# A message-passing kernel: the first half of the filter layer ahead of the sums, in layer 0

## The chip, the cores and the metric

The kernel runs on one core of a Trainium2 chip. The metric is the device time of one execution in microseconds. The engines are TensorE (PE in the profile, its weight loads PEld), VectorE (DVE), ScalarE (ACT), GpSimd (POOL) and SyncE (SP); they run side by side and order themselves with semaphores only.

## What is computed

A graph of 12,500 nodes and 412,500 edges, sorted by destination, goes through two layers. The part that matters here:

```python
# layer 0
msg = edge_weight[:, None] * x[src]
agg = segment_sum(msg, dst, num_segments=N)
h = relu((x + agg) @ W1 + b1)
x = layernorm(x + (h @ W2 + b2))
# layer 1, on the new x
h1 = x @ lin1_w.T
z = softplus(edge_attr @ nn_w1.T + nn_b1) - log(2)      # "filter layer 1": depends on the edges alone
W = (softplus(z @ nn_w2.T + nn_b2) - log(2)) * c[:, None]
msg = W * h1[dst]                                       # summed over src
```

The first filter layer doesn't depend on `x`, so the kernel computes it during layer 0's pass over the edges and stores it for layer 1.

## The kernel before

**Stages.** After some preparation comes the pass over the edges of layer 0, in T = 403 tiles of 1024 edges, then layer 0's node stage, then the pass over the edges of layer 1 and its node stage. The change lies in the first pass alone (the engines' programs from line 352 on). The edges are sorted by destination, so a tile touches few nodes; a "window" is 42 nodes (WIN), and each tile runs an inner loop over its windows (one for each tile with these inputs: a tile issues eight gathers per window, and 3224 are issued).

**What each engine does in tile t**, in the order of its program; each engine works off its own queue in order:

- *GpSimd* (L420 to 437): for each window eight indirect gathers (`xg[s]`, s = 0 to 7, 128 rows of `x` each, L432). Gather s waits until the indices `gidx` are there and until the sum that read `xg[s]` in the window before is over (`summed`). Each `xg[s]` is one buffer.
- *ScalarE* (L402 to 416): copies the indices `gidx` for the window's gathers in two halves (L411), each when the gathers of the window before that used that half have landed; then `soft_1(t, 0)` and `soft_1(t, 1)` (L395, L397, L399: Abs, Exp, Ln), on the filter results of tile t-1.
- *TensorE* (L454 to 481): the counts (L463, L465: sixteen small bf16 matmuls on `oha`, which VectorE makes at the start of its tile; `counted`); then the window loop: wait for `flushed` and for the one-hots, and eight sums (L475), each after its gather has landed, into `bank[0]`, each an increment of `summed`. Then the two halves of the first filter layer (L481), `attr` times `nn1`, 512 columns in fp32 each, into `bank[2]` and `bank[3]` (`z1_set`). Half h waits for the tile's `attr` load and for `hid_set >= taken_up(t, h)`: VectorE's `hidden(t, h)` must have read the bank's last contents.
- *VectorE* (L545 to 596): `rel`, `oha`; in the window loop it waits for all sums of the window before, makes eight one-hots (L563), adds `bank[0]` of the window before to `aggT` (L499), and steps `rel`; then the ranks of the tile: `pair` (L574), `ahead` (L578, which waits for the counts), `count` (L580, L584), `seen` (L582), `rank` (L587); then `hidden(t, 0)` (L506), a bucket count (L699, in three of four parts), and `hidden(t, 1)`. Each `hidden` combines the filter result of tile t-1 with ScalarE's output and increments `hid_set`.
- *SyncE* (L366 to 376): loads `attr` for tile t (L371) when both halves of t-1 are done; stores `hid` (L363) when `hidden(t, 1)` is done; clears a block of the table for layer 1 (L376).

`attr`, `hid`, the one-hots and each bank named above are single buffers. The counts of what is before: `z1_set` starts at 2 by two matmuls on zeros, `hid_set` at 2, `summed` at 8. From these, `made(k, h)` = 2k + h + 1 and `taken_up(k, h)` = 2k + h + 3.

Of the kernel before, what the change touches and what calls it, by code (L numbers as in the profile page):

```python
# [51 lines left out]
def edge_network_kernel(nc, x_rows, x_cols, src_cols, dst_cols, w_cols, dst_rows,  # L52
# [8 lines left out]
    with ctx:  # L61
        def sb(name, shape, dt):
            return ctx.enter_context(nc.sbuf_tensor(name, shape, dt))

        def sem(name):
            return ctx.enter_context(nc.semaphore(name))
# [45 lines left out]
        nn1 = sb("nn1", [P, D], f32)  # L112
        b1c = sb("b1c", [P, 1], f32)
        bank = [ctx.enter_context(nc.psum_tensor(f"bank{i}", [P, 512], f32)) for i in range(8)]
# [6 lines left out]
        with ExitStack() as c0:  # L121
# [28 lines left out]
            with nc.Block() as block:  # L150
                @block.sync
                def _(sp):
                    for i in range(NGRP):
                        sp.dma_start(rows_i[0:g[i], i, :], dst_rows[P * i:P * i + g[i], :]).then_inc(dst_in[i], 16)
                    sp.dma_start(wgt[:, :], w_cols).then_inc(w_in, 16)
                    sp.wait_ge(s_win, 1)
                    sp.dma_start(base_d[:, :].rearrange("(i p) o -> p i o", p=P), least[:, :].rearrange("p (i o) -> p i o", o=1), allow_slow_non_contiguous=True).then_inc(win_st, 16)
                    sp.dma_start(nwin_d[:, :].rearrange("(i p) o -> p i o", p=P), most[:, :].rearrange("p (i o) -> p i o", o=1), allow_slow_non_contiguous=True).then_inc(win_st, 16)
                    sp.wait_ge(win_st, 32)
                    sp.dma_start(base[:, 0:T], base_d[0:T, :].rearrange("t o -> o t").broadcast_to([P, T])).then_inc(s_tab, 16)  # L160
                    sp.dma_start(nwin[:, 0:T], nwin_d[0:T, :].rearrange("t o -> o t").broadcast_to([P, T])).then_inc(s_tab, 16)
                    for i in range(NGRP):
                        sp.wait_ge(dst_half, i + 1)
                        sp.dma_start(dst16[P * i:P * i + g[i], :], rows_h[0:g[i], i, :]).then_inc(s_st, 16)
                    sp.wait_ge(s_st, 16 * NGRP)
                    sp.wait_ge(s_tab, 32)
# [137 lines left out]
        with ExitStack() as c1:  # L304
# [3 lines left out]
            with ExitStack() as c2:  # L308
                def sb2(name, shape, dt):
                    return c2.enter_context(nc.sbuf_tensor(name, shape, dt))  # L310
# [9 lines left out]
                attr = sb2("attr", [P, 2, HE], f32)  # L320
# [17 lines left out]
                attr_padded, attr_in = sem("attr_padded"), sem("attr_in")  # L338
                z1_set, abs1, exp1, ln1, hid_set = (sem(n) for n in ("z1_set", "abs1", "exp1", "ln1", "hid_set"))
# [8 lines left out]
                def taken_up(k, h):  # L348

                    return 2 * k + h + 3  # L350

                with nc.Block() as block:
# [85 lines left out]
                    @block.tensor  # L438
                    def _(pe):
                        def plan_part(q):  # L440

                            pe.wait_ge(bucket_counts, NB + q * PT)
                            nc.tensor.matmul(bank[5][0:NB, 0:1], counts[:, 0:NB], ones[:, 0:1], start=True, stop=True).then_inc(planned, 1)
                            pe.wait_ge(plan, PLAN_STEPS * q + 3)
                            nc.tensor.matmul(bank[5][:, 128:128 + NB], blocks[0:NB, :], before_col[0:NB, :], start=True, stop=True)
                            nc.tensor.matmul(bank[5][:, 256:256 + NB], blocks[0:NB, :], upto[0:NB, :], start=True, stop=True)
                            nc.tensor.matmul(bank[5][0:NB, 384:385], upto[0:NB, :], blocks[0:NB, 0:1], start=True, stop=True).then_inc(planned, 1)
                            pe.wait_ge(plan, PLAN_STEPS * q + 5)
                            nc.tensor.matmul(bank[4][:, 0:SLOTS], ones16[0:NB, :], at_or_past[0:NB, :], start=True, stop=True).then_inc(planned, 1)

                        nc.tensor.matmul(bank[0][:, 0:WIN], lower[:, :], zero16[:, 0:WIN], start=True, stop=True).then_inc(summed, SUB)
                        for h in range(2):
                            nc.tensor.matmul(bank[2 + h][:, :], ident[:, :], zero[:, 0:HE], start=True, stop=True).then_inc(z1_set, 1)
                        pe.sem_inc(counted, 1)  # L454
                        jobs = TileTable(pe, "pe0", nwin)
                        for q, first, past_last in parts:
                            plan_part(q)
                            with pe.Fori(first, past_last) as t:
                                windows = jobs.windows()
                                pe.wait_ge(oha_set, t + 1)  # L460
                                pe.wait_ge(seen_set, t + 1)
                                for s in range(SUB):
                                    nc.tensor.matmul(above, lower[:, :], oha[:, s, :], start=(s == 0), stop=(s == SUB - 1))  # L463
                                for s in range(SUB):
                                    ins = nc.tensor.matmul(in_tile, ones16[:, :], oha[:, s, :], start=(s == 0), stop=(s == SUB - 1))  # L465
                                ins.then_inc(counted, 1)
                                with pe.Fori(0, windows):
                                    j = jobs.number()
                                    pe.wait_ge(flushed, j + 2)
                                    pe.wait_ge(onehot_ready, j + 1)  # L470
                                    for s in range(SUB):
                                        if s == HALF:
                                            jobs.read_ahead(t)
                                        pe.wait_ge(gathered[s], 16 * (j + 2))
                                        nc.tensor.matmul(bank[0][:, 0:WIN], xg[s][:, :], onehot[:, s, :],  # L475
                                                         start=(s == 0), stop=(s == SUB - 1)).then_inc(summed, 1)
                                    jobs.step()
                                for h in range(2):
                                    pe.wait_ge(attr_in, 16 * (t + 1))
                                    pe.wait_ge(hid_set, taken_up(t, h))  # L480
                                    nc.tensor.matmul(bank[2 + h][:, :], nn1[:, :], attr[:, h, :], start=True, stop=True).then_inc(z1_set, 1)  # L481

                    @block.vector
                    def _(dve):
# [973 lines left out]
```

## Time and profile before

| | |
|---|---|
| Median of 3 runs | 9315.23 us (9307.72 to 9319.87) |
| The profiled execution | 9315.85 us, of which the span is 9314.2 us |
| Busy, share of the span | PE 65%, PEld 52%, DVE 70%, ACT 37%, POOL 68% |
| Layer 0's gathers | 3224, from 158.0 to 4368.7 us of the span |
| TensorE's mean granted clock | 0.74 of full speed; 0.70 from 1000 to 4000 us |
| DMA | 1533 MB, mean 165 GB/s |

Shares of busy time are means over stages with different limits, so the rows below are of the stage that the change touches. In them PE matmuls are grouped with their neighbours of the same kind ("x6" is six, or three fp32 products of two passes each), times are us from the start of the span, and a bracket at the end of a line is the idle time of that engine just before it and what ended it.

### The profile page before, as it was taken

Reading aid. Unit: us, or ns where it says so; the run is one execution under the profiler, and the core shown is the slowest. Engines: PE = TensorE matmul, PEld = TensorE weight load, DVE = VectorE, ACT = ScalarE, POOL = GpSimd, SP = SyncE. Lnnn points to the kernel's source line nnn. Section 1 sums busy time; section 2 is a strip of 40 time slices with the busy share of each in tenths; the row PEclk is TensorE's granted clock in tenths of the full one; section 3 lists DMA queues with packets and bytes.
Section 4 is the critical chain, followed back from the end, with each engine's and each line's share of the span. In section 5 each row is a group of like instructions: output and inputs, shape, how many; then the busy total and the mean of one; then the engine's idle time right before and its main releaser. Section 6 shows DMA issues by size and latency. Waiting matters only on the chain. (4 is left out here: it accounts for less than half of the span.)

```text
span 9314.2 us, 204001 instructions
## 1 busy us (share of the span) xinstructions
PE 6033.2 (65%) x35189; PEld 4808.1 (52%) x35190; DVE 6494.6 (70%) x20428; ACT 3471.8 (37%) x6781; POOL 6297.2 (68%) x6541
## 2 busy tenths in 40 slices
PE   2666666666666666666655556666666666666676
PEld 1444444444444444444444446666666666666665
DVE  7777777777777776665655556777777777777655
ACT  2333333333333333333544443333333333333202
POOL 2777777777777777775277777777777777777400
PEclk8676766776767667776855557888888888888887
DMA  3444444444444444444444446666666666666554
GB/s 101 148 146 147 148 144 146 149 146 143 146 149 147 145 145 148 149 147 142 143 134 134 134 134 199 208 210 206 205 206 208 209 207 206 205 207 207 174 167 147
DMA packets 803241, 1533.30 MB, mean 165 GB/s; under 512 B 193070, under 2 KB 206820, under 8 KB 802707
## 3 DMA queue, kind: packets, MB, share of 16 engines
q1 hardware_dynamic: 593415, 1093.58, 36.2%
q0 software_dynamic: 209456, 436.16, 15.7%
q10 hardware_dynamic: 348, 3.33, 0.1%
q14 instruction: 16, 0.13, 0.0%
q8 instruction: 6, 0.10, 0.0%
HBM read 967.92 MB, written 564.58 MB: 165 GB/s over the span
## 5 line engine op out<-in xcount | busy, mean ns | idle before, releaser
L1204 POOL DMA_INDIRECT sorted_messages<-rows,sidx x3224 | 3212.4, 996 | 1154.7 <-issue 932.4
L432 POOL DMA_INDIRECT xg<-x_rows,gidx x3224 | 3043.0, 944 | 1306.8 <-issue 1020.2
L475 PE MATMUL bank<-onehot,xg 128*128 128x42 f32 x6448 | 1116.6, 326 | 1400.4 <-DMA xg<-x_rows,gidx 1386.2
L475 PEld LDWEIGHTS bank<-onehot,xg 128*128 128x128 f32 x6448 | 1004.2, 233 | 1474.0 <-DMA xg<-x_rows,gidx 1457.1
L1132 PE MATMUL bank<-hot,block_rows 128*128 128x128 f32 x9312 | 1576.2, 347 | 145.4 <-DVE hot L1286 145.1
L1132 PEld LDWEIGHTS bank<-hot,block_rows 128*128 128x128 f32 x9312 | 1530.3, 260 | 169.2 <-issue 154.0
L481 PE MATMUL bank<-attr,nn 128*128 128x512 f32 x1612 | 1453.7, 1057 | 3.0 <-DVE hid L506 3.0
L1102 PE MATMUL bank<-w_nn2T,e_hid 128*128 128x128 f32 x6448 | 1039.0, 314 | 162.2 <-DMA e_hid<-hidden 162.1
L1102 PEld LDWEIGHTS bank<-w_nn2T,e_hid 128*128 128x128 f32 x6448 | 1007.8, 226 | 245.3 <-DMA e_hid<-hidden 212.1
L1113 PE MATMUL bank<-h1w,ohT 128*128 128x128 bf16 x3224 | 349.4, 275 | 1069.6 <-DVE ohT L1233 1066.4
L1257 DVE SCALAR_TENSOR_TENSOR rows<-filt,meta,bank 128x128 f32<-128x128 f32 x3224 | 904.7, 343 | 94.7 <-DVE filt L1248 47.2
L563 DVE TENSOR_SCALAR onehot<-cols,rel,wgt 128x42 f32<-128x42 f32 x3224 | 734.8, 327 | 233.2 <-PE bank L475 230.5
L1286 DVE TENSOR_TENSOR hot<-cols,block_rows 128x512 f32<-128x512 f32 x1167 | 800.2, 686 | 118.0 <-DMA block_rows<-sorted_messages 117.5
L1113 PEld LDWEIGHTS bank<-h1w,ohT 128*128 128x128 bf16 x3224 | 266.7, 123 | 1144.4 <-issue 1144.2
L395 ACT ACTIVATE soft<-bank 128x512 f32<-128x512 f32 x808 | 474.8, 588 | 1008.5 <-PE bank L481 1004.0
L1166 ACT ACTIVATE rows<-meta 128x4 f32 (+1 forms) x806 | 167.4, 208 | 1743.0 <-DMA sorted_messages<-rows,sidx 1743.0
L1248 DVE SCALAR_TENSOR_TENSOR filt<-bank,soft 128x512 f32<-128x512 f32 x806 | 555.0, 689 | 344.7 <-issue 188.3
L1157 ACT ACTIVATE soft<-bank 128x512 f32<-128x512 f32 x806 | 481.2, 597 | 734.9 <-PE bank L1102 553.3
L411 ACT ACTIVATE gidx<-srci 128x4 int32 x806 | 165.5, 205 | 1543.2 <-DMA xg<-x_rows,gidx 1357.7
L481 PEld LDWEIGHTS bank<-attr,nn 128*128 128x128 f32 x1612 | 483.2, 329 | 422.5 <-issue 411.4
L1297 DVE TENSOR_TENSOR aggT<-aggT,bank 128x128 f32 x1164 | 328.9, 283 | 435.6 <-issue 258.9
L506 DVE SCALAR_TENSOR_TENSOR hid<-bank,soft 128x512 f32<-128x512 f32 x808 | 542.9, 682 | 4.6 <-ACT soft L399 4.6
(180 smaller groups left out, 7427.8 us busy)
## 6 DMA issues: line engine op xcount, KB each, us to landing
block_rows<-sorted_messages SPq DMA_DIRECT2D x389, 792.0 KB
hidden<-hid SPq DMA_DIRECT2D x404, 512.0 KB
e_hid<-hidden SPq DMA_DIRECT2D x403, 512.0 KB
sorted_messages<-zero SPq DMA_DIRECT2D x403, 264.0 KB
dstb<-dst SPq DMA_DIRECT2D x403, 256.0 KB
attr<-attr_cols SPq DMA_DIRECT2D x403, 204.0 KB
xg<-x_rows,gidx POOLq DMA_INDIRECT x3224, 4.2
sorted_messages<-rows,sidx POOLq DMA_INDIRECT x3224
```

The source lines that it names most:

```text
L432: pool.indirect_dma_start(xg[s][:, :], None, x_rows, bass.IndirectOffsetOnAxis(ap=gidx[s // HALF][:, s % HALF:s % HALF + 1], axis=0),).the ...
L475: nc.tensor.matmul(bank[0][:, 0:WIN], xg[s][:, :], onehot[:, s, :], start=(s == 0), stop=(s == SUB - 1)).then_inc(summed, 1)
L481: nc.tensor.matmul(bank[2 + h][:, :], nn1[:, :], attr[:, h, :], start=True, stop=True).then_inc(z1_set, 1)
L506: dve.scalar_tensor_tensor(hid[:, h, :], bank[2 + h][:, :], 0.0, soft1[h][:, :], ALU.max, ALU.add).then_inc(hid_set, 1)
L563: ins = dve.tensor_scalar(onehot[:, s, :], cols[:, 0:WIN], rel[:, s:s + 1], wgt[:, ds(here + s, 1)], ALU.is_equal, ALU.mult)
L1102: ins = nc.tensor.matmul(bank[2 + h][:, s * P:s * P + P], hid[:, h, s * P:s * P + P], nn2T[:, :], start=False, stop=(s == HALF - 1))
L1113: ins = nc.tensor.matmul(bank[4 + h][:, s * P:s * P + P], ohT[:, at:at + P], h1w[:, :], start=True, stop=True)
L1132: ins = nc.tensor.matmul(sums[u][:, 0:P], block_rows[k][:, u, s, 0:D], hot[u][:, s, :], start=(s == 0), stop=(s == HALF - 1))
L1204: pool.indirect_dma_start(table, bass.IndirectOffsetOnAxis(ap=sidx[b][h][:, s:s + 1], axis=0), rows[b][h][:, s, :], None).then_inc(landed[ ...
L1248: dve.scalar_tensor_tensor(filt[h][:, :], bank[2 + h][:, :], 0.0, soft2[h][:, :], ALU.max, ALU.add).then_inc(filt_set, 1)
L1257: ins = dve.scalar_tensor_tensor(rows[b][h][:, s, 0:D], filt[h][:, part], meta[:, ds(here + (h * HALF + s), 1), 1], bank[4 + h][:, part], ...
L1286: dve.tensor_tensor(hot[u][:, :, :], cols[:, :].rearrange("p (o n) -> p o n", o=1).broadcast_to([P, HALF, P]), block_rows[k][:, u, :, D:D ...
```

## The change

TensorE's first filter layer is put into a function, and half 0 is issued right after the tile's counts, ahead of the window loop with the sums of gathered rows. Half 1 stays behind the sums. Each half takes its two waits with it. Nothing else differs.

```diff
+                        def first_layer(t, h):
+
+                            pe.wait_ge(attr_in, 16 * (t + 1))
+                            pe.wait_ge(hid_set, taken_up(t, h))
+                            nc.tensor.matmul(bank[2 + h][:, :], nn1[:, :], attr[:, h, :], start=True, stop=True).then_inc(z1_set, 1)
+
...
                                 ins.then_inc(counted, 1)
+                                first_layer(t, 0)
                                 with pe.Fori(0, windows):
                                     j = jobs.number()
                                     pe.wait_ge(flushed, j + 2)
...
                                     jobs.step()
-                                for h in range(2):
-                                    pe.wait_ge(attr_in, 16 * (t + 1))
-                                    pe.wait_ge(hid_set, taken_up(t, h))
-                                    nc.tensor.matmul(bank[2 + h][:, :], nn1[:, :], attr[:, h, :], start=True, stop=True).then_inc(z1_set, 1)
+                                first_layer(t, 1)
```

## Rows read from the trace of the kernel before

**Rows 1.** The gathers' line, 1000 to 4000 us: count, durations, landing.

```profile
L432 POOL DMA_INDIRECT xg<-x_rows,gidx x2300: 938/944/1000, 999.4 to 3999.4; - x192
...
DMA to landing us min/median/max: 2.4/4.1/7.2
```

**Rows 2.** The page's group of the same line, over the whole span.

```profile
L432 POOL DMA_INDIRECT xg<-x_rows,gidx x3224 | 3043.0, 944 | 1306.8 <-issue 1020.2
```

**Rows 3.** Waits, 1000 to 4000 us: total us, times, longest us.

```profile
PE bank L475 <- DMA xg<-x_rows,gidx: 991.9, 387, 4.6
...
ACT soft L395 <- PE bank L481: 713.6, 286, 7.9
...
PEld bank L481 <- DVE hid L506: 5.5, 6, 1.2
```

**Rows 4.** Timeline, 2000 to 2022 us, all engines: start, length, engine, line.

```profile
2004.59 1.51 PE L475 MATMUL bank<-onehot,xg 128*128 128x42 f32 x6 [3.09 <-DMA xg<-x_rows,gidx]
...
2005.89 3.34 PE L481 MATMUL bank<-attr,nn 128*128 128x512 f32 x4
...
2006.24 1.78 DVE L563 TENSOR_SCALAR onehot<-cols,rel,wgt 128x42 f32<-128x42 f32 x8 [0.81 <-PE bank L475]
...
2009.12 0.22 DVE L574 TENSOR_TENSOR pair<-bucket 128x64 f32 x1 [0.90 <-issue]
...
2009.41 0.33 SPq L371 DMA_DIRECT2D attr<-attr_cols  x1
...
2009.79 1.34 PE L475 MATMUL bank<-onehot,xg 128*128 128x42 f32 x10
...
2009.99 0.27 DVE L578 TENSOR_TENSOR bank<-bank,seen 128x100 f32<-128x100 f32 x1 [0.64 <-PE bank L465]
...
2011.93 0.94 POOL L432 DMA_INDIRECT xg<-x_rows,gidx  x1 [0.30 <-issue]
2012.17 0.20 ACT L411 ACTIVATE gidx<-srci 128x4 int32 x1 [0.46 <-issue]
2012.61 0.68 DVE L506 SCALAR_TENSOR_TENSOR hid<-bank,soft 128x512 f32<-128x512 f32 x1
...
2013.27 0.94 POOL L432 DMA_INDIRECT xg<-x_rows,gidx  x1 [0.40 <-issue]
...
2015.21 1.27 PE L475 MATMUL bank<-onehot,xg 128*128 128x42 f32 x6 [4.08 <-DMA xg<-x_rows,gidx]
...
2015.76 0.20 ACT L411 ACTIVATE gidx<-srci 128x4 int32 x1 [3.38 <-DMA xg<-x_rows,gidx]
```

**Rows 5.** Timeline, 170 to 275 us: the first tile, where TensorE waited for `hid`.

```profile
174.53 3.64 PE L475 MATMUL bank<-onehot,xg 128*128 128x42 f32 x16 [8.84 <-DVE aggT L499]
...
175.24 0.23 DVE L574 TENSOR_TENSOR pair<-bucket 128x64 f32 x1 [0.86 <-issue]
...
175.99 0.94 POOL L432 DMA_INDIRECT xg<-x_rows,gidx  x1 [8.11 <-PE bank L475]
...
178.03 0.68 DVE L506 SCALAR_TENSOR_TENSOR hid<-bank,soft 128x512 f32<-128x512 f32 x1
...
178.77 3.78 PE L481 MATMUL bank<-attr,nn 128*128 128x512 f32 x4 [0.60 <-DVE hid L506]
```

**Rows 6.** Busy time by stretch: PE, PEld, DVE, ACT, POOL, then granted PEclk.

```profile
2008.00:2009.00 1.00, 1.00 (x2) 0.22 (x2) 0.23 (x3) 0.97 (x2) 0.82 (x1) 0.66 0.55 197
...
2015.00:2016.00 1.00, 0.79 (x5) 0.79 (x6) 0.89 (x1) 0.20 (x1) 0.69 (x2) 0.75 0.20 62
```

**Rows 7.** DMA queues, 2014.0 to 2014.5 us: packets, MB, share of 16 engines.

```profile
q1 hardware_dynamic: 4, 0.01, 5.8%
```

## Prediction

> **What bounds the kernel now.** I read the gathers' own line first, then the table of waits, then one tile in order of time. The reader is to see one stage, the pass over the edges in layer 0. [rows 1] has 2300 gathers from 999.4 to 3999.4 us; at eight to a tile of 1024 edges that is 3000.0 / 2299 x 8 = **10.44 us per tile**. The whole kernel issues 3224 of them [rows 2], 403 tiles of one window each. A gather is 0.94 us and its issue gap 0.30 us [rows 1, 4], so the GpSimd stream alone would take 8 x 1.25 = 10.0 us; the rest is its short waits. [rows 3] says who waits in those 287.5 tiles: TensorE stands 991.9 us for gathered rows (3.4 us a tile), ScalarE 713.6 us for the filter layer (2.5 us a tile), and TensorE almost never for `hid` (5.5 us in all). That last row is the one that the change touches.
>
> [rows 4] is one tile, t. TensorE ends the sums of t-1 at 2004.59 + 1.51 = 2006.10, runs both filter matmuls of t-1 (from 2005.89, 3.34 us), then the counts of t, and at 2009.79 five of the eight sums of t, whose rows are there. Then it idles 4.08 us until the last three arrive at 2015.21. VectorE starts the one-hots of t at 2006.24, 0.14 us after the sums of t-1, goes through add, `pair` (2009.12), `ahead`, `count`, `rank`, and only at 2012.61 reaches `hidden(t, 0)`, which ends at 2013.29. GpSimd's gathers for t+1 begin at 2013.27; the buffers had been free since the five sums.
>
> **What changes, part by part.** Nothing is added or removed: 403 first-half filter matmuls (fp32, 512 columns) move past the sums, with both their waits. (a) `attr_in` for t: see (d). (b) `hid_set >= taken_up(t, 0)`, which is 2t + 3 with 2 given at the start: it is reached by `hidden(t, 0)` of the same tile, not of the one before. VectorE comes to it at the end of its tile. So TensorE, done with the counts before 2009.99 (where `ahead` is released [rows 4]), would stand until 2013.29, and **behind it in its queue stand all eight sums of t**. Who waits for those: GpSimd (each gather of t+1 needs its buffer back) and VectorE (the one-hots of t+1 need all sums of t).
>
> (c) That closes a ring which before was open: sums(t-1) -> VectorE's whole tile up to `hidden(t, 0)` -> first filter matmul -> sums(t). Its length:
> - sums end to one-hots: 0.14 us (2006.10 to 2006.24 [rows 4]).
> - one-hots to `pair`: 2.88 us (2006.24 to 2009.12 [rows 4]).
> - `pair` to the end of `hidden(t, 0)`: in the tile of [rows 4] it contains a wait for the counts; in [rows 5], where there was none, it is 175.24 to 178.03 + 0.68, 3.47 us. I take this one, as the counts will follow a single filter matmul and come in time.
> - `hid` to TensorE: 178.71 to 178.77, 0.06 us [rows 5].
> - first filter matmul: half of the pair, between 3.34 / 2 [rows 4] and 3.78 / 2 [rows 5] at the low clock; 1.8 us. At full clock about 0.9.
> - eight sums: 16 matmuls in 3.64 us at the low clock [rows 5], 0.455 us a sum; at the full clock ten in 1.34 us [rows 4], 0.27 us a sum. Which of them? The burst of [rows 4] starts at 2004.59 after an idle stretch; the granted clock is 0.66 over 2008 to 2009 [rows 6], that is 0.5 (1.2 GHz) to about 2008.7 and then 1.0 (2.4 GHz): 4.1 us from the start of the burst. In the changed kernel the burst begins with the filter matmul after about as long an idle stretch; so 1.8 us of filter, 2.3 us or five sums at the low clock, three at the full: 1.8 + 2.3 + 0.8 = 4.9 us. Bounds: 0.9 + 2.2 = 3.1 (all full), 1.8 + 3.64 = 5.4 (all low).
>
> Sum: 0.14 + 2.88 + 3.47 + 0.06 + 4.9 = **11.45 us per tile**; bounds 9.65 and 12.0.
>
> A second ring goes through GpSimd and two tiles. From the end of sums(t-1) the first sum of t is over after 0.14 + 2.88 + 3.47 + 0.06 + 1.8 + 0.45 = 8.8 us. A gather held by a sum starts 1.0 us after it (sum over at 174.53 + 0.455, gather at 175.99 [rows 5]); held by `gidx`, 0.9 us (2012.37 to 2013.27 [rows 4]). The eighth starts 7 x 1.25 = 8.75 us later, lands after 3.8 us (2011.93 to ScalarE's `gidx` at 2015.76 [rows 4]; the median of all is 4.1 [rows 1]), and its sum takes 0.3 to 0.45. Two tiles are 8.8 + 1.0 + 8.75 + 3.83 + 0.4 = 22.8 us, **11.4 a tile**; 10.9 with the filter matmul and the sums at the full clock.
>
> Two rings of equal length, with landings from 2.4 to 7.2 us [rows 1], give more than either: I add 0.2 us, an estimate, and take **11.65 us per tile**.
>
> (d) The other waits. The load of `attr` is issued once both halves of the tile before are done (2009.41 in [rows 4], 0.18 us after the pair's end at 2009.23); its queue, q1, still has 4 packets at 2014.0 to 2014.5 [rows 7], so it lands about 4.9 us after issue. In the changed kernel: sums end + 0.9 (1.8 if the clock is low) + 0.2 + 4.9 = 6.0 to 6.9, against 6.55 at which `hid` comes. Usually hidden by VectorE's tile; with a low clock it adds 0.35 us. It is past no other DMA on SP's queue, as store, clearing and load keep their order. ScalarE gains: its 2.5 us wait for the first half [rows 3] goes, since that result is there before the gathers land. What is late next is not ScalarE but the sums, so this is worth nothing. The second half keeps its place; `hidden(t, 1)` has ended 1.7 us after `hidden(t, 0)`, long before it. Other stages don't change.
>
> **The sum.** (11.65 - 10.44) x 403 = 488 us. The profiled execution took 9315.85 us (span 9314.2), level with the median of the runs, 9315.23; so 9315.85 + 488 = **9804 us**, 5.2% slower.
>
> **Rivals.**
> 1. *The clock stays full* through the burst. TensorE's idle stretch might shrink or shift so that the fall after it (clock 0.75 over 2015 to 2016, so falling just as the burst starts, [rows 6]) doesn't come. Then the VectorE ring is 9.65, the GpSimd ring 10.9 us a tile and decides: 9315.85 + 0.46 x 403 = 9500 us. Against it: idle is 11.6 less some 7 us of work, over 4 us, as now. The Trainium skill, "TensorE: Matmul & The Clock Gate", section "Why this matters for your kernels", tells us to avoid long TensorE gaps between bursts to hold the clock; by it a filter matmul set into the gap could pay. In [rows 4] the matmul can't start until the gap is nearly over.
> 2. *The clock stays low* through the sums and `attr` is late: 12.0 + 0.35 = 12.35 us, 9315.85 + 1.91 x 403 = 10,086 us. For it: the sums stream only 42 columns and are short; against it, the clock rose in bursts that held such sums.
> 3. *Faster.* ScalarE's 2.5 us freed, `gidx` is ready early, and GpSimd runs without waits at 10.0 to 10.1 us a tile: 9315.85 - 0.35 x 403 = 9175 us. It decides if `hidden(t, 0)` ends before TensorE has done the counts, at or before 2009.99; it ends 3.3 us after.
> 4. *No change*: the 1.8 us fit into TensorE's idle 4.08 us, 2013.35 to 2015.15, just ahead of the last three sums, 9316 us. It would hold if GpSimd had spare buffers; but its gather for t+1 at 2013.27 needs the first sum of t, which would end only at 2015.6.
>
> **How the numbers follow.** Forecast (11.3 to 12.0 us a tile, 9662 to 9944 us) 0.68; rival 1 0.12; rival 2 0.13; rival 3 0.04; rival 4 0.03. The range leaves out the two last and the upper part of rival 2: 9490 to 10,060. Within 0.2%, about what a measurement can tell from no change, 0.03; faster 0.04; slower 0.93.
>
> **What would show it.** In the changed kernel's rows: TensorE waits for `hid` (VectorE line of `hidden`) some 3 to 4 us a tile, and for gathers little; all eight sums stand together after a filter matmul; GpSimd waits for the sums about 1.2 us a tile; ScalarE's wait for the filter layer goes down; gathers are 11.3 to 12.0 us apart by eights, and the time from the last gather to the end is unchanged. Wrong would be: TensorE's wait for `hid` small, or GpSimd still at 1.25 us throughout.

## The result and the profile after

The changed kernel takes **10311.48 us** (10300.55 to 10323.45) against 9317.55 us for the kernel before, a ratio of 1.107 with a 95% interval of 1.105 to 1.108. The direction was right, the size was not: 994 us more where 488 were forecast, and outside the range.

The profile after, the page: the groups of the gathers and of the filter layer (now L455).

```profile
L432 POOL DMA_INDIRECT xg<-x_rows,gidx x3224 | 3042.2, 944 | 2296.5 <-PE bank L482 1515.5
...
L455 PE MATMUL bank<-attr,nn 128*128 128x512 f32 x1612 | 1662.3, 1135 | 1768.2 <-DMA attr<-attr_cols 1578.3
```

The gathers are as long as in [rows 2]; GpSimd's idle time before them has grown from 1306.8 to 2296.5 us, by 989.7 us, and the span has grown by 989.3 us (10303.5 against 9314.2). The whole loss is in this one stage.

The gathers' line of the changed kernel, 1000 to 4000 us, to set beside [rows 1]:

```profile
L432 POOL DMA_INDIRECT xg<-x_rows,gidx x1857: 938/944/971, 999.9 to 3999.3; - x186
```

Eight gathers are (3999.3 - 999.9) / 1856 x 8 = **12.93 us** apart, against 10.44 before; 2.49 x 403 = 1003 us. (All periods below are worked out in this way.)

The waits of the same stretch, for [rows 3]:

```profile
PE bank L455 <- DMA attr<-attr_cols: 960.0, 220, 5.3
POOL xg L432 <- PE bank L482: 877.0, 682, 10.3
DVE onehot L567 <- PE bank L482: 873.3, 231, 4.6
PEld bank L455 <- DVE hid L510: 775.2, 173, 5.5
```

TensorE no longer waits for gathered rows: the table has no such row for it. It waits some 4 us a tile ahead of the first half, and the rows disagree on whom for: its weight load is released by `hid`, the matmul itself by the `attr` load, which came last in 220 of 232 tiles. GpSimd and VectorE wait for the sums.

One tile of the changed kernel, timeline 2000 to 2030 us, for [rows 4]:

```profile
2004.16 3.48 PE L482 MATMUL bank<-onehot,xg 128*128 128x42 f32 x16
...
2007.43 2.06 PE L455 MATMUL bank<-attr,nn 128*128 128x512 f32 x2
...
2009.67 0.32 SPq L371 DMA_DIRECT2D attr<-attr_cols  x1
...
2013.54 0.68 DVE L510 SCALAR_TENSOR_TENSOR hid<-bank,soft 128x512 f32<-128x512 f32 x1
...
2014.98 2.07 PE L455 MATMUL bank<-attr,nn 128*128 128x512 f32 x2 [4.15 <-DMA attr<-attr_cols]
...
2016.84 3.48 PE L482 MATMUL bank<-onehot,xg 128*128 128x42 f32 x16
```

This is the ring, with all its links: sums end 2007.64; 2.03 us of second half until the load goes out; 5.31 us until the first half starts; 1.86 us until the sums start; 3.48 us of sums, ending at 2020.32. Sum **12.68 us**; the stage's mean of 12.93 holds longer loads too (the next one goes out at 2022.35, and TensorE starts at 2028.33, 5.98 us later). `hid` is ready at 2014.22, 0.76 us before the first half starts: the forecast's VectorE ring is there, but the load closes a longer one around it.

The granted clock through that burst (columns as in [rows 6]):

```profile
2009.00:2010.00 1.00, 1.00 (x10) 0.72 (x9) 0.84 (x5) 0.47 (x1) 0.79 (x1) 0.50 0.24 66
...
2011.00:2012.00 1.00, 0.00 (x0) 0.00 (x0) 1.00 (x4) 0.45 (x1) 0.70 (x2) 0.73 0.32 66
...
2013.00:2014.00 1.00, 0.00 (x0) 0.00 (x0) 1.00 (x2) 0.00 (x0) 0.90 (x1) 1.00 0.39 127
```

TensorE's work from 2002.30 to 2010.8 runs wholly at 0.5 (1.2 GHz). In this tile the clock rises to 1.0 (2.4 GHz) in 2011 to 2012, when the burst is over, and is high while TensorE waits; in the next wait, from 2023.6 to 2028.3, it stays at 0.50. Why it differs is open. The low clock in the bursts isn't this tile's alone. The durations of all 1612 filter matmuls (two make a half; ns, min/median/max), the kernel before and then the changed one:

```profile
L481 PE MATMUL bank<-attr,nn x1612: 593/1061/1222, 178.8 to 4376.0; 128*128 128x512 f32 x180
```

```profile
L455 PE MATMUL bank<-attr,nn x1612: 1057/1087/1223, 178.2 to 5364.9; 128*128 128x512 f32 x180
```

The short ones, run at the high clock, are gone: none is under 1057 ns.

### The profile page after: what moved, and what is told of

Same layout as the page of the kernel before. It is cut to its first block and busy times, and to the rows that moved or that the text cites. A ratio compares the mean times of both kernels' runs of the same rounds, so it can differ in the third digit from the quotient of the medians.

```text
span 10303.5 us, 204001 instructions
## 1 busy us (share of the span) xinstructions
PE 6657.4 (65%) x35189; PEld 5383.8 (52%) x35190; DVE 6501.5 (63%) x20428; ACT 3518.0 (34%) x6781; POOL 6302.5 (61%) x6541
## 5 line engine op out<-in xcount | busy, mean ns | idle before, releaser
L432 POOL DMA_INDIRECT xg<-x_rows,gidx x3224 | 3042.2, 944 | 2296.5 <-PE bank L482 1515.5
L455 PE MATMUL bank<-attr,nn 128*128 128x512 f32 x1612 | 1662.3, 1135 | 1768.2 <-DMA attr<-attr_cols 1578.3
L482 PEld LDWEIGHTS bank<-onehot,xg 128*128 128x128 f32 x6448 | 1475.0, 334 | 416.3 <-issue 416.3
L482 PE MATMUL bank<-onehot,xg 128*128 128x42 f32 x6448 | 1402.2, 411 | 0.0
L455 PEld LDWEIGHTS bank<-attr,nn 128*128 128x128 f32 x1612 | 422.3, 322 | 1848.9 <-DVE hid L510 1492.2
L469 PEld LDWEIGHTS bank<-oha,lower 128*128 128x128 bf16 x3224 | 322.3, 147 | 499.1 <-issue 486.4
```

The source lines that it names most:

```text
L432: pool.indirect_dma_start(xg[s][:, :], None, x_rows, bass.IndirectOffsetOnAxis(ap=gidx[s // HALF][:, s % HALF:s % HALF + 1], axis=0),).the ...
```

## The experiments

Three things were to be told apart: the wait for `hid`, the wait for the `attr` load, and the clock. The kernel before ran beside each group of experiments and had medians from 9300 to 9353 us, so kernels of different groups are compared by their ratios; a point is 1% of the kernel before, 93 us. The groups are the change; e1 to e4; e5 to e8; e9 and e10; e11; e12; e13 and e14.

| kernel | us | ratio to before, 95% interval |
|---|---|---|
| the change | 10311 | 1.1067 (1.1053 to 1.1081) |
| e1 split load | 9962 | 1.0662 (1.0644 to 1.0680) |
| e2 added matmuls | 9810 | 1.0502 (1.0481 to 1.0523) |
| e3 split load, added matmuls | 9513 | 1.0182 (1.0165 to 1.0199) |
| e4 both halves ahead | 10634 | 1.1382 (1.1363 to 1.1401) |
| e5 second bank | 10346 | 1.1074 (1.1050 to 1.1098) |
| e6 second bank, split load | 9343 | 0.9995 (0.9984 to 1.0006) |
| e7 split load, `hidden` early | 9426 | 1.0074 (1.0053 to 1.0096) |
| e8 before, added matmuls | 9679 | 1.0359 (1.0328 to 1.0390) |
| e9 e6, load earlier | 9167 | 0.9795 (0.9782 to 0.9809) |
| e10 e9, three added matmuls | 9172 | 0.9805 (0.9792 to 0.9819) |
| e11 e9's loads, order of before | 9538 | 1.0207 (1.0193 to 1.0221) |
| e12 e11, store not held | 9189 | 0.9834 (0.9812 to 0.9856) |
| e13 e3 with half the added work | 9631 | 1.0352 (1.0336 to 1.0367) |
| e14 before, split load | 9235 | 0.9931 (0.9918 to 0.9945) |

### e1: the load of half 0 earlier

The semaphore `attr_in` becomes one for each half, and TensorE's wait ahead of half h goes by `attr_in[h]`. SyncE's part:

```diff
-                                sp.wait_ge(z1_set, made(t, 1))
-                                sp.dma_start(attr[0:GAUSS + 1, :, :].rearrange("a h e -> a (h e)"), attr_cols[:, ds(t * TE, TE)]).then_inc(attr_in, 16)
+                                for h in range(2):
+                                    sp.wait_ge(z1_set, made(t, h))
+                                    sp.dma_start(attr[0:GAUSS + 1, h, :], attr_cols[:, ds(t * TE + h * HE, HE)]).then_inc(attr_in[h], 16)
```

> The changed kernel, with the attr load split in two: half 0 for tile t is loaded as soon as the first filter matmul of t-1 is done, some 5 us before half 1. In the changed kernel TensorE starts the first half 0.76 us after hid is there (2014.22 to 2014.98), and the wait ends with the attr load. Theory attr (the load is the last to come): the first half starts with hid, and the ring at the low clock is 0.14 + 6.44 + 0.06 + 1.86 + 3.48 = 12.0 us a tile instead of 12.93, so 10311 - 0.93 x 403 = 9940 us. Theory VectorE (hid alone holds it, the load comes just with it): no change, 10311 us. The clock stays at 0.5 in the bursts in both.

Measured 9962 us; the theory of the load had said 9940. The waits of e1, 1000 to 4000 us:

```profile
PE bank L456 <- DVE hid L511: 891.3, 249, 5.1
```

Now `hid` ends the wait in all 249 tiles, and gathers by eights are 12.06 us apart, which is the forecast's VectorE ring with the clock low (12.0). The load was worth 12.93 - 12.06 = 0.87 us a tile, 350 us, or 4.05 points by the ratios.

### e2 and e3: the clock

```diff
                                 ins.then_inc(counted, 1)
+                                for k in range(8):
+                                    nc.tensor.matmul(bank[1][:, :], ones16[:, :], bucket16[:, 0:HE], start=True, stop=True)
                                 first_layer(t, 0)
```

> The changed kernel, with eight bf16 matmuls of 512 columns on TensorE after the counts, into a bank that nobody reads, in the 4 us in which it waits for hid and attr. Theory clock (half of the loss is that the burst runs at 1.2 GHz): the granted clock of the stage goes from 0.57 to over 0.9, the first half takes 0.9 us instead of 1.86, a sum 0.27 instead of 0.43, the attr load is issued 0.9 us earlier; the VectorE ring is 0.14 + 6.44 + 0.06 + 3.1 = 9.75 us and GpSimd's two-tile ring gives 10.5 to 10.9: 9340 to 9500 us. Theory ring (the clock matters little beside the waits): within 100 us of 10311. If the added matmuls hold the clock but come in the way of the first half, 0.2 to 0.5 us a tile more.

> Both edits. Theory clock and ring: with the clock full GpSimd's two-tile ring decides, so the split load adds next to nothing, 9300 to 9480 us. Theory attr as the larger part: below the fill alone by over 200 us.

Measured 9810 and 9513 us. The added work is eight bf16 matmuls of 512 columns whose results nobody reads. It does nothing but keep TensorE busy in part of its wait, and takes 5.65 points off the changed kernel and 448 us, 4.8 points, off e1. The stretch 1000 to 4000 us of the changed kernel, of e2 and of e3, in that order:

```profile
1000.00:4000.00 3000.00, 1970.98 (x8372) 1400.83 (x8371) 1853.54 (x5130) 956.43 (x1856) 1751.82 (x1857) 0.57 0.36 118
```

```profile
1000.00:4000.00 3000.00, 2224.38 (x11052) 1440.58 (x11279) 2019.45 (x5611) 1048.55 (x2045) 1933.12 (x2045) 0.76 0.41 130
```

```profile
1000.00:4000.00 3000.00, 2267.47 (x11865) 1463.92 (x12115) 2147.83 (x5982) 1119.34 (x2199) 2076.55 (x2196) 0.79 0.45 140
```

The mean clock goes from 0.57 to 0.76 and 0.79. It did not reach the expected 0.9, and neither time the 9340 to 9500 that went with it: in e2's timeline the first half takes 1.12 us and the second, behind the sums, again 2.05.

```profile
2003.39 1.12 PE L455 MATMUL bank<-attr,nn 128*128 128x512 f32 x2 [3.56 <-DMA attr<-attr_cols]
...
2008.33 2.05 PE L455 MATMUL bank<-attr,nn 128*128 128x512 f32 x2
```

So the clock falls within the burst: the granted clock is 1.00 in 2004 to 2005 and 0.51 in 2005 to 2006. The split load, worth 4.05 points without the added work, was worth 296 us (3.2 points) with it. That is e3's second theory (over 200 us), not its first (next to nothing): the two-tile ring through GpSimd wasn't the bound, since the load still came last in 215 tiles of e2 (waits, 1000 to 4000 us).

```profile
PE bank L455 <- DMA attr<-attr_cols: 563.4, 215, 5.1
```

### e13: half the added work

The same loop with `range(4)`.

> e3 with four added matmuls instead of eight. Theory that any work right behind the counts keeps the clock up through the wait for hid: as e3, 9500 us. Theory that the clock's share grows with the work added: between, 9650 to 9850 us. Theory that four are not enough to bring a rise in time for the burst: as e1, 9960 us.

Measured 9631 us, a ratio of 1.0352 against e1's 1.0662 and e3's 1.0182: 3.1 of e3's 4.8 points for half the work. That lies between, as the middle theory had it, if just under its 9650 to 9850 us. Its mean clock over 1000 to 4000 us lies between too: 0.65, against 0.57 in e1 and 0.79 in e3.

### e4: both halves ahead of the sums

```diff
                                 first_layer(t, 0)
+                                first_layer(t, 1)
...
-                                first_layer(t, 1)
```

> Both halves of the filter layer ahead of the sums. TensorE then waits for hidden(t, 1) too, 1.7 us later. Theory VectorE ring with the clock low throughout: 0.14 + 8.15 + 0.06 + 1.86 + 3.48 = 13.7 us a tile, 10,620 us. Theory that the clock rises only behind two filter matmuls in a row: they are in a row again, the sums or most of them run at the full clock, 12.4 to 12.8 us a tile, 10,100 to 10,260 us, and the stage's mean clock is above 0.65. The attr load isn't late, as it goes out before the sums.

Measured 10634 us, 13.70 us a tile. One theory was that the clock rises when two filter matmuls stand in a row, as before the change. It doesn't: they stand in a row here, and the stage's mean clock is the lowest of all.

```profile
1000.00:4000.00 3000.00, 1816.97 (x7902) 1306.02 (x7900) 1747.49 (x4839) 878.27 (x1752) 1652.22 (x1751) 0.51 0.35 112
```

The VectorE ring with the later `hidden(t, 1)` and the low clock had been worked out as 13.7 us, and it is 13.70.

### e5 and e6: a second bank, so that `hid` is not waited for

Half 0 goes to `bank[2]` and `bank[1]` in turn; engines run over pairs of tiles. In TensorE's part:

```diff
-                            pe.wait_ge(hid_set, taken_up(t, h))
-                            nc.tensor.matmul(bank[2 + h][:, :], nn1[:, :], attr[:, h, :], start=True, stop=True).then_inc(z1_set, 1)
+                            pe.wait_ge(hid_set, made(t, 0) if h == 0 else taken_up(t, 1))
+                            nc.tensor.matmul(z1_bank(h, b)[:, :], nn1[:, :], attr[:, h, :], start=True, stop=True).then_inc(z1_set, 1)
```

> The changed kernel with a second bank for half 0, taken in turn by even and odd tiles, so that the first filter matmul of t waits for hidden(t-1, 0), one tile back, and no more for hidden(t, 0). The attr load is one transfer, as in the changed kernel. Theory that each of the two waits alone makes a ring: sums end, second half and its attr issue 2.0, load 4.9 to 5.3, first half and sums at the low clock 5.3: 12.2 to 12.7 us a tile, 10,030 to 10,230 us. Theory VectorE ring alone: with hid gone the loss goes, 9300 to 9500 us.

> The second bank and the split attr load together: TensorE's first half then waits for nothing of its own tile. Every theory in which the two waits carry the loss: back at GpSimd's stream, 10.0 to 10.5 us a tile, 9200 to 9400 us. Theory that the order on TensorE itself (a filter matmul ahead of sums, at a low clock) costs something: over 9500 us.

These are the sharpest pair. With the wait for `hid` gone and the load as in the change, e5 takes 10346 us: nothing is gained. With the load split as well, e6 takes 9343 us, the time of the kernel before (0.9995). e5's waits, 1000 to 4000 us:

```profile
PE bank L459 <- DMA attr<-attr_cols: 934.3, 210, 6.2
```

So each wait is enough by itself for a ring: the load alone for the whole loss (13.00 us a tile; 12.2 to 12.7 had been expected) and `hid` alone (e1) for 6.6%. With both eased, e6 is level with the kernel before. That doesn't make the new order free, since e6 has a second bank and a split load, which the kernel before lacks. e12, below, has both, and SyncE's queue in the same order; it differs from e6 only in that half 0 stands behind the sums again, and it takes 9189 us (0.9834). The new order thus still costs 1.6 points in e6, where TensorE waits for the load in 223 of 284 tiles (1000 to 4000 us):

```profile
PE bank L460 <- DMA attr<-attr_cols: 480.0, 223, 5.0
```

### e7: `hidden(t, 0)` earlier on VectorE

e1, with `hidden(t, 0)` right behind the window loop instead of behind the ranks.

```diff
+                                hidden(t, 0)
                                 dve.tensor_tensor(pair[:, :, :], wide(bucket16[:, ds(here, SUB)], SUB), tall(bucket16[:, ds(here, SUB)], SUB),
...
-                                hidden(t, 0)
```

> The changed kernel with the split attr load, and VectorE's hidden(t, 0) moved from behind the ranks to right behind the window loop, 3.3 us earlier. The VectorE ring is 0.14 + 2.9 + 0.68 + 0.06, then 5.34: 9.1 us, and GpSimd's stream of 10.0 us or VectorE's own tile of some 10.0 to 10.4 us decides: 9250 to 9450 us. Against e1 (9962 us) this tells that the place of hidden in VectorE's tile carries the rest of the loss. If it does not, 9960 us.

Measured 9426 us, 5.9 points less than e1: it is the place of `hidden` at the end of VectorE's tile that makes the second ring long.

### e8: the added work in the kernel before

The eight added matmuls of e2, ahead of the sixth sum, in the kernel before.

> The kernel before with eight bf16 matmuls of 512 columns that nobody reads, ahead of the sixth sum, in TensorE's 4 us of waiting for rows. The clock of the stage goes from 0.70 to over 0.9. Since GpSimd's stream of 10.0 us a tile bounds, this is worth at most the 0.44 us above it: 9190 to 9350 us. A theory by which TensorE's clock is what bounds the kernel before would have it under 9150 us.

Missed: 9679 us, 3.6% slower, though the mean clock over 1000 to 4000 us went from 0.70 to 0.77. Timeline of e8:

```profile
2002.84 3.19 PE L476 MATMUL bank<-bucket,ones 128*128 128x512 bf16 x7 [0.22 <-issue]
...
2005.83 1.35 PE L478 MATMUL bank<-onehot,xg 128*128 128x42 f32 x6
```

In this tile the added work was not in the wait for rows but behind it: it started late, ran at the low clock, and the last three sums stood behind it until 2005.83, though the rows of all eight had landed before 2002.66, when ScalarE copied the next indices. Over 1000 to 4000 us VectorE's wait for the sums goes from 158.2 to 468.0 us. So a higher mean clock is no gain in itself; that the late sums are the whole of e8's loss is read from this tile and this wait, and no run shows it by itself.

### e9 and e10: a version that beats both

e6, and SyncE loads half 0 of t+1 before it waits to store `hid` of t:

```diff
+                            load_attr(t, 1)
+                            if more:
+                                load_attr(t + 1, 0)
                             store_hidden(t)
```

> e6 (second bank, split load), and half 0's load for tile t+1 moved on SyncE's queue ahead of the store of hid and the clearing of tile t, so that it goes out right behind the first filter matmul of t. In e6 TensorE still waits for attr in 223 of 284 tiles, 480 us in 1000 to 4000 us, since the load stands behind the store and the clearing. Theory that this rest is what keeps e6 from gaining over the kernel before: GpSimd's waits for the sums go, 10.1 to 10.3 us a tile, 9200 to 9290 us. Theory that GpSimd's stream and its own short waits bound e6: no change, 9340 us.

> e9 with three bf16 matmuls of 512 columns that nobody reads, ahead of the sixth sum. The clock of the stage goes up from 0.6; at the full clock the three take 0.65 us, at the low 1.3. If the low clock still costs something in e9, 20 to 100 us less than e9; if GpSimd's stream bounds, no change; if the added work comes in the way of the last sums as in e8, 50 to 150 us more.

e9 takes **9167 us, 2.05% less than the kernel before**. Its gathers' line:

```profile
L445 POOL DMA_INDIRECT xg<-x_rows,gidx x2382: 939/945/1000, 1000.1 to 4000.0; - x199
```

That is 10.08 us a tile, next to the 10.0 of GpSimd's stream alone, and the time is below the 9200 to 9290 us expected. e10 adds nothing (9172 us) though its mean clock is 0.72 against e9's 0.68 (1000 to 4000 us), as its theory that GpSimd's stream bounds had it.

### e11, e12 and e14: what e9's gain is due to

e11 is e9 with both halves behind the sums; e12 moreover has the load of half 0 for t+1 behind the store and the clearing.

> e9 with one thing put back: both halves behind the sums, as in the kernel before, with the second bank and the early loads kept. Theory that e9's gain comes from the half ahead of the sums (ScalarE's work then doesn't wait for it, and the gathers' indices for the next tile come earlier): about the kernel before, 9300 to 9400 us. Theory that it comes from the bank or the loads whatever the order: 9160 to 9200 us.

> e11 with the load of half 0 for t+1 behind the store and the clearing of t on SyncE's queue, so that nothing stands behind its wait: both halves behind the sums, second bank, split loads. In e11 the store of hid stood behind that wait, and VectorE waited for the store. Theory that e9's gain over the kernel before needs the half ahead of the sums: 9300 to 9400 us. Theory that bank and loads give it in any order: 9160 to 9220 us.

> The kernel before with the split attr load alone. e12 gained 1.7% over the kernel before with its order kept. Theory that the split load is what gave it (two transfers of 102 KB at different times stand less in the way of the gathers): 9170 to 9210 us. Theory that it was the second bank and the loops over pairs of tiles: 9340 us.

e11 (9538 us) met neither of its theories and was no clean comparison. It put a new wait in: SyncE's queue, and the store of `hid` in it, stood behind the first half, and VectorE waited for that store.

```profile
DVE hid L524 <- DMA hidden<-hid: 114.4, 179, 1.5
```

That row is 114.4 us in some 272 tiles (1000 to 4000 us), only a part of what e11 loses against e12; e12 differs in the place of that load alone. It takes 9189 us, which refutes the theory that the gain needs the new order: 1.66 of the 2.05% come with the order of before. e14, the split load alone in the kernel before, takes 9235 us and gives 0.69%, between its two theories (9170 to 9210 us, and 9340 us). e12 has e14's loads in e14's order, so the rest of its gain lies in the second bank or the loops over pairs of tiles; no run separates these. The 0.4 points between e12 and e9 belong to the new order and the earlier load together. Each change alone is a loss: from e12, the new order alone gives e6 (1.6 points slower), the earlier load alone e11 (3.7 points slower).

## Why the prediction was wrong

**Where the time goes** (right in the main). The stage, the ring through `hidden(t, 0)`, the eight sums standing behind it, and that GpSimd and VectorE would wait for them were as put. GpSimd's wait was put too short, though: 1.2 us a tile, and it is 877.0 us in 232 tiles, 3.8. And ScalarE has no gain at all: its wait for the filter layer, which was to go, is 769.5 us in 232 tiles (1000 to 4000 us), 3.3 us a tile against 2.5. From the start of the last gather to the end of the span it is 9314.2 - 4368.7 = 4945.5 us before and 10303.5 - 5358.1 = 4945.4 us after (timeline of GpSimd), so nothing changed behind the stage.

**The VectorE ring** (right in its links). Its low-clock bound was 12.0; e1, which has only this ring, measured 12.06, and e4 13.70 for 13.7.

**Part (d), the load** (the step that failed). It was set at 6.0 to 6.9 us from the end of the sums, against 6.55 for `hid`, and called usually hidden. Measured: 2.03 + 5.31 = 7.34 us. Two of its terms were off, both to the same side: the second half was taken at 0.9 us with the clock high, and takes 2.06; and the landing at 4.9 us, where 5.31 us pass from issue to TensorE's start. The load then is the last to come in 220 of 232 tiles, and costs 0.87 us a tile (the change against e1). The forecast had worked out this very sum for rival 2, which it priced at 12.35 us a tile and gave 0.13; its price, too, was 0.6 short, and its 10,086 us already lay outside the range given.

**The clock** (the second term). For the burst a rise after 4.1 us was carried over from [rows 6], since idle times would be alike. They are (4.15 us against 4.08), and still the burst of 8.5 us ran wholly at the low clock. That moves the ring from 11.45 to 12.0. So the sum comes out: 11.45, 0.61 for the clock (12.06 in e1) and 0.87 for the load are 12.93 us a tile. The two errors are tied, by this sum: it is the low clock behind the sums that makes the load go out late. e2 and e3 show that 5.65 and 4.8 points of what was measured can be had back by added work that raises the mean clock. That is an effect of the added work as a whole, its own cost included; nothing in their rows but the clock speaks for a gain from it, and it didn't reach the full clock. Why the clock rose in time before and not after is **not settled**: the theory of two filter matmuls in a row fell with e4. The Trainium skill, "TensorE: Matmul & The Clock Gate", section "Why this matters for your kernels", warns of gaps between bursts. e3 and e13 agree with it so far as work added in the gap raised the mean clock and took 4.8 and 3.1 points off; e8 shows that the advice has its price.

**The allowance.** The 0.2 us for two rings of equal length was no substitute for working out the third. The GpSimd ring wasn't the bound in the changed kernel, where TensorE never waits for rows, and the gathers land in 2.5 us in the median (1000 to 4000 us), where 4.1 was seen before. The price of that ring at the full clock was also off by 0.1: 7.7 + 1.0 + 8.75 + 3.83 + 0.3 = 21.6 us for two tiles, 10.8 a tile and not 10.9, so that rival 1 comes to some 9460 us, below the range.

**The rivals.** The faster one and the one without change were rightly held unlikely in this kernel. Rival 3's first link does come about once both waits are released: in e9 ScalarE's wait for the filter layer is 82.6 us (1000 to 4000 us), and the new order stands in the fastest kernel. It is worth little: e12, with the order of before and 708.8 us of that wait, is 0.4 points slower.

## What to carry to other kernels

When an instruction moves up an in-order queue, work out for each of its waits a full ring through the queue, by the slowest clock that the trace shows, and take the longest; two waits that end close together will hide each other in an experiment too, so release them together as well as one at a time. A load that was issued "when the buffer is free" was safe only because its reader came late: a move of the reader makes the issue point of the load the next thing to move. And put back the old order once the mended version is fast, as e12 did: most of the gain may be in the mending.

## What the runs showed of the hardware that was not expected

A burst of 8.5 us, with TensorE busy throughout, ran at a granted clock of 0.5 to its end, and the clock was 1.0 only in the idle time behind it, and not in the idle time after the next burst; before the change it had risen 4.1 us into the burst. In e13, a smaller dose of added work than in e3 gave a mean clock (0.65) between e1's 0.57 and e3's 0.79.

And the same 204 KB of `attr`, loaded as two transfers instead of one, made the kernel before 0.69% faster (e14), where no engine had been waiting for `attr`. Why is not shown.
